# Graph layers with two layer norms: four of ten dense rows' second sums on ScalarE, and a one-row last slot

## Chip, cores and metric

One core of one Trainium2 chip. The time is device microseconds of the whole program; less is better.

## The reference, cut to what matters

A graph of 50000 nodes with 128 features and 12500 edges. A first message layer gives x1 = layernorm(x + mean of messages), then two relational attention layers (eight relations, softmax over each node's incoming edges) and x2 = layernorm(x1 + h2):

```python
x = _layernorm(x + _L0_gnn_ref(x, edge_attr_128, src, dst, ...), axis=-1)
x = _layernorm(x + _L1_gnn_ref(x, W, att_q, att_k, bias, edge_index, edge_type_8), axis=-1)
```

Most nodes have no incoming edge. For such a row the messages are zero and each attention layer gives relu(bias), so the output is layernorm(layernorm(x) + relu(bias of layer 1)). This is the dense work: it runs over all 50000 rows beside the edge work, and rows with edges are overwritten at the end.

## The kernel before

**Dense work.** The rows are cut into 39 slots (c = 0 to 38) of 10 rows on each of 128 partitions (BR = 10) and a last slot c = 39 (BC) with one row on 80 partitions. Three buffers of `stage` hold slots in turn. Step k does the first layer norm of slot k and the second of slot k - 1:

- VectorE `bulk_first(k)`: five pair statistics (one instruction gives count, mean and summed square deviation of two rows) of slot k, once its load has landed.
- VectorE `bulk_shift(k)`: waits for `b_norm1`, adds relu(bias) to all rows of slot k - 1.
- VectorE `bulk_second(k)`: five pair statistics of slot k - 1; then `b_sum`.
- ScalarE `root(k)`: square root of all twenty sums; then `b_sd`.
- VectorE `bulk_scales(k)`: a reciprocal and a product give scale `rs` and bias `nm`; then `b_rs`.
- ScalarE `bulk_norm(k, 0)`: ten norms (one per row, scale and bias) of slot k, then `b_norm1`; `bulk_norm(k, 1)`: ten of slot k - 1, then `b_norm2`.
- SyncE `bulk_step(k)`: waits for `b_norm2`, stores slot k - 1, waits for the store, loads slot k + 2 in its place.

In the before kernel the last slot is treated as ten rows on every engine but in its load and store.

**Edge work.** 98 tiles of 128 edges in 14 groups of 7 (NG = 14, G = 7). First stage: groups 0 to 13 with dense steps 3 to 16. Then two attention layers (j = 0, 1). A layer runs over 112 slots n; for n < 98, group g = n // 7, r = n % 7 + 1. In slot n:

- VectorE makes mask r of group g (`STT(masked(n), ...)`, into one of three buffers; it waits until TensorE has used the mask three slots back), then the dense piece of that r (`bulk_piece`), then, in some slots, a piece of the softmax (`chain`, slots 38 to 45 and 66 to 73) and every fourth slot from 50 the weighting and running sum of a group (`weighted`).
- TensorE multiplies mask r with the relation's matrix (`product`; relation 0 goes first in a group, from the rows themselves). At slots 4, 9, 14, ... it turns the rows of the next group (`turn_rows`, needs the gather), and two slots later makes its key scores (`key_scores`).
- ScalarE copies turned rows (`rows_T`), key scores (`keys_out`) and, at r = 7, the group's products (`products_out`) out of PSUM, and does the dense norms and roots at fixed r; from slot 50 also `relu_sums`, `h1_out` and `fill`.
- GpSimd gathers the rows of all groups in one run (98 indirect transfers, each group into its own place).

Each engine's queue runs in program order. Layer 0 has dense steps k = 18 to 30 in groups 0 to 12, layer 1 steps 33 to 39 in groups 0 to 6 and the last, 40, in group 7. Steps 17, 31 and 32 lie ahead of the layers' slots. Before, the dense pieces stand so:

- VectorE: r 1 and 2 `bulk_first`, 3 shift, 4 `bulk_second` and sums, 6 scales.
- ScalarE: r 2 and 3 the second norms of step k - 1 (five each), 4 root, 6 and 7 the first norms of step k.
- SyncE: its step at r 4.

## Time and profile before

| | |
|---|---|
| median of 3 runs | 950.29 us (945.18 to 953.65) |
| profiled execution | 952.45 us, span 950.7 us |
| busy: PE, DVE, ACT, POOL | 678.6, 750.2, 614.4, 581.1 us |
| layer 0, its slots | about 335 to 616 us |
| layer 1, its slots | about 632 to 913 us |

PE is TensorE, DVE VectorE, ACT ScalarE, POOL GpSimd. Times in the trace count from the span's start. In a timeline row stand start, duration, engine, line, operation, written<-read tile, count, and in brackets the idle time before it and who ended it. Instructions of one kind in a row are merged, and successive ones overlap a little, so a pace is read from start to start.

### The profile page before, as it was taken

Reading aid. Unit: us, or ns where it says so; the run is one execution under the profiler, and the core shown is the slowest. Engines: PE = TensorE matmul, PEld = TensorE weight load, DVE = VectorE, ACT = ScalarE, POOL = GpSimd, SP = SyncE. Lnnn points to the kernel's source line nnn. Section 1 sums busy time; section 2 is a strip of 40 time slices with the busy share of each in tenths; the row PEclk is TensorE's granted clock in tenths of the full one; section 3 lists DMA queues with packets and bytes.
Section 4 is the critical chain, followed back from the end, with each engine's and each line's share of the span. In section 5 each row is a group of like instructions: output and inputs, shape, how many; then the busy total and the mean of one; then the engine's idle time right before and its main releaser. Section 6 shows DMA issues by size and latency. Waiting matters only on the chain.

```text
span 950.7 us, 10537 instructions
## 1 busy us (share of the span) xinstructions
PE 678.6 (71%) x3022; PEld 431.6 (45%) x3022; DVE 750.2 (79%) x1445; ACT 614.4 (65%) x1425; POOL 581.1 (61%) x506
## 2 busy tenths in 40 slices
PE   2646756656475499997998689649998888678810
PEld 2524544545353355554665345426564455343400
DVE  3488877887679678978998899688978887899950
ACT  1569898989799766656566687566665564334450
POOL 4777777777771488887700000088888866557774
PEclk9657696777767589999998999869999999889955
DMA  8276657656563422323553454523231521142210
GB/s 226 87 215 200 204 161 220 206 170 200 161 186 123 157 71 97 101 70 125 195 148 114 127 185 142 166 87 110 69 129 45 184 70 48 42 113 81 70 41 29
DMA packets 87764, 122.96 MB, mean 129 GB/s; under 512 B 14188, under 2 KB 66854, under 8 KB 87707
## 3 DMA queue, kind: packets, MB, share of 16 engines
q1 hardware_dynamic: 69483, 99.36, 33.4%
q0 software_dynamic: 15680, 21.55, 8.1%
q10 hardware_dynamic: 2544, 1.38, 0.7%
q8 instruction: 24, 0.39, 0.2%
q14 instruction: 33, 0.27, 0.1%
HBM read 87.79 MB, written 45.05 MB: 140 GB/s over the span
## 4 chain that ended last, share of the span: by engine, by line
DVE 27%; POOL 22%; issue 17%; PE 14%; ACT 11%; DMA 7%; SPq 1%; POOLq 0%; DVEq 0%; ACTq 0%
POOL xs L471 16%; DVE ys L1145 5%; PE ps_y L727 5%; DVE work L1320 5%; POOL xd L471 4%; ACT stage L808 4%; DVE st L1073 4%; DMA xs<-h_table,posI 3%; DVE ys L1292 2%; DVE opT L1320 2%; PE ps_t L689 2%; PE ps_t L588 2%; ACT xd L824 1%; POOL out L540 1%; DMA xs<-x_table,posI 1%
## 5 line engine op out<-in xcount | busy, mean ns | idle before, releaser
L808 ACT ACTIVATE stage<-stage,nm,rs 128x128 f32<-128x128 f32 x800 | 319.9, 483 | 19.1 <-DVE nm L1069 19.1
L727 PE MATMUL ps_y<-work,wr 128*128 128x512 f32 (+1 forms) x528 | 231.8, 572 | 20.0 <-DVE work L1320 20.0
L471 POOL DMA_INDIRECT xs<-h_table,posI x98 | 130.1, 1327 | 169.3 <-DMA h_table<-ys 139.7
L471 POOL DMA_INDIRECT xs<-x_table,posI x98 | 128.0, 1306 | 61.1 <-DMA x_table<-xd 31.5
L1073 DVE BATCH_NORM_STATS2 st<-stage 128x6 f32<-128x256 f32 x400 | 144.6, 418 | 25.1 <-DMA stage<-in_x 23.8
L1320 DVE SCALAR_TENSOR_TENSOR work<-typB,xs 128x896 f32<-128x896 uint8 x132 | 142.6, 1087 | 18.4 <-ACT xs L773 9.0
L727 PEld LDWEIGHTS ps_y<-work,wr 128*128 128x128 f32 x528 | 100.4, 200 | 115.1 <-issue 70.8
L540 POOL DMA_INDIRECT out<-xd,outI x98 | 107.8, 1100 | 55.0 <-issue 27.7
L471 POOL DMA_INDIRECT xs<-in_x,srcI x98 | 103.7, 1058 | 43.3 <-issue 28.7
L471 POOL DMA_INDIRECT xd<-in_x,dstG x98 | 109.7, 1119 | 29.9 <-issue 28.6
L727 PE MATMUL ps_y<-opT,wr 128*128 128x512 f32 (+1 forms) x256 | 114.9, 573 | 10.3 <-DVE opT L1320 10.3
L824 ACT ACTIVATE xd<-xd,nm,rs 128x128 f32<-128x128 f32 x196 | 78.3, 481 | 18.1 <-DVE nm L1069 18.1
L1145 DVE TENSOR_TENSOR_SCAN ys<-sameB,tail,ys 128x896 f32<-128x896 uint8 x39 | 81.2, 2081 | 0.9
L1320 DVE SCALAR_TENSOR_TENSOR opT<-typB,xs 128x896 f32<-128x896 uint8 x64 | 69.7, 1089 | 10.1 <-PE ps_y L727 8.1
L727 PEld LDWEIGHTS ps_y<-opT,wr 128*128 128x128 f32 x256 | 48.3, 200 | 55.1 <-issue 33.5
L773 ACT ACTIVATE xs<-ps_t 128x896 f32<-128x896 f32 x28 | 25.7, 916 | 73.1 <-PE ps_t L677 73.1
L1086 DVE TENSOR_TENSOR stage<-stage,relu_row 128x1280 f32<-128x1280 f32 x40 | 59.4, 1485 | 6.9 <-ACT stage L808 6.9
L1068 DVE RECIPROCAL rs<-sd 128x20 f32<-128x20 f32 (+3 forms) x55 | 15.3, 277 | 57.5 <-ACT sd L802 57.1
L727 PE MATMUL ps_y<-xs,wr 128*128 128x512 f32 (+1 forms) x112 | 51.9, 589 | 2.2 <-ACT xs L773 2.2
L717 PEld LDWEIGHTS ps_k<-wqk,xs 128*128 128x128 f32 x392 | 47.9, 192 | 6.2 <-issue 0.6
L623 PE MATMUL ps_y<-opT,mixed 128*128 128x512 f32 (+1 forms) x56 | 36.2, 737 | 15.3 <-ACT opT L773 15.3
L905 ACT ACTIVATE ys<-ys,bcol 128x896 f32<-128x896 f32 x28 | 29.2, 1043 | 27.4 <-DVE tail L1148 27.0
(208 smaller groups left out, 1027.6 us busy)
## 6 DMA issues: line engine op xcount, KB each, us to landing
stage<-in_x SPq DMA_DIRECT2D x39, 640.0 KB, 4.2
out<-stage SPq DMA_DIRECT2D x39, 640.0 KB, 3.0
xs<-alpha_rows SPq DMA_DIRECT2D x28, 448.0 KB, 4.7
x_table<-xd SPq DMA_DIRECT2D x14, 448.0 KB, 3.0
h_table<-ys SPq DMA_DIRECT2D x14, 448.0 KB, 3.4
work<-in_src SPq DMA_DIRECT2D x13, 448.0 KB, 5.5
ys<-in_edge_attr SPq DMA_DIRECT2D x6, 896.0 KB, 9.2
sameB<-same_rows SPq DMA_DIRECT2D x42, 112.0 KB, 3.7
```

The lines of the kernel that those rows point to most:

```text
L471: nc.gpsimd.indirect_dma_start(out=buf[:, t, :], out_offset=None, in_=table, in_offset=bass.IndirectOffsetOnAxis(ap=idx[:, t:t + 1], axis= ...
L540: nc.gpsimd.indirect_dma_start(out=out, out_offset=bass.IndirectOffsetOnAxis(ap=outI[:, t:t + 1], axis=0), in_=xd[:, t, :], in_offset=None ...
L623: pe.matmul(ps_y[:, 0, lo:hi], m_node, opT[:, 0, lo:hi], start=True, stop=False)
L717: mm = pe.matmul(ps_k[:, t * R:(t + 1) * R], xs[:, g * G + t, :], wqk[:, 1, j * R:(j + 1) * R], start=True, stop=True)
L727: mm = pe.matmul(ps_y[:, u, lo:hi], wr[:, r, :], rows, start=(r == 0), stop=(r == R - 1))
L808: ins = a.activation(slot(c)[:, r, :], slot(c)[:, r, :], ACT.Identity, bias=nm[:, h, n:n + 1], scale=rs[:, h, n:n + 1])
L824: ins = a.activation(buf[:, g * G + t, :], buf[:, g * G + t, :], ACT.Identity, bias=nm[:, h, o + t:o + t + 1], scale=rs[:, h, o + t:o + t ...
L905: a.activation(cols_of(ys, g), cols_of(ys, g), ACT.Relu, bias=bcol[:, 5 + j:6 + j]).then_inc(g_act[j], 1)
L1073: return v.bn_stats(st[:, h, o:o + 2, :].rearrange("p a c -> p (a c)"), both)
L1086: T.of(TT(slot(k - 1), slot(k - 1), mid(relu_row[:, 1, :], BR), ALU.add))
L1145: ins = scan(cols_of(ys, g), sameB[:, n % 2, :], cols_of(ys, g), tail[:, 0:1] if g else 0.0, ALU.mult, ALU.add)
L1320: STT(masked(n), typB[:, m % 2, :], float(r), cols_of(xs, g), ALU.is_equal, ALU.mult).then_inc(m_mask[j], 1)
```

## The change

Four things. (1) In steps 18 to 39 the last four rows (SQ = 4) of slot k - 1 get no pair statistic. ScalarE squares them with a running sum (`bulk_squares`), from the shift on (`b_shift`), before the root, into the place where the summed square deviation would stand. (2) That is the deviation only if the shifted row's mean is zero, so relu(bias) has its mean taken off once in the prologue; those rows' second norm then has no bias. (3) The order in a layer's group: VectorE's scales go from r 6 to 7. ScalarE has squares at 4, root at 5, second norms at 7 (five) and at r 1 of the next group (five), first norms, all ten, at r 2. SyncE's step goes from r 4 to 2. (4) The last slot: one statistic, one row shifted and one norm in place of ten rows.

```diff
@@ -193,6 +196,12 @@
             b = c % SLOTS
             return stage[:, b * BR * D:(b + 1) * BR * D].rearrange("p (r d) -> p r d", d=D)
 
+        def rows_of(c):
+            return 1 if c == BC else BR
+
+        def squared(k):
+            return SQ if K_H[0] < k <= BC else 0
+
         def grp(t, g):
             return t[:, g * G:g * G + G, :]
 
@@ -247,6 +256,7 @@
         pro = sem("dve_steps")
 
         b_sum = sem("b_sum"); b_sd = sem("b_sd"); b_rs = sem("b_rs"); b_norm1 = sem("b_norm1"); b_norm2 = sem("b_norm2")
+        b_shift = sem("b_shift"); b_sq = sem("b_sq")
 
         p_step = sem("p_step"); p_row = sem("p_row"); p_ready = sem("p_ready")
 
@@ -419,7 +429,7 @@
                     bulk_step(k)
                 for n in range(SLOTS_ALL):
                     g, r = n // (R - 1), n % (R - 1) + 1
-                    if r == 4 and K_M[j] + g <= K_E[j]:
+                    if r == 2 and K_M[j] + g <= K_E[j]:
                         bulk_step(K_M[j] + g - 1)
                     if n in STORE:
                         alpha_store(j, STORE.index(n))
@@ -803,21 +813,36 @@
 
             def bulk_norm(k, half, rows=range(BR)):
                 h, c, done = k % 2, k - half, (b_norm1, b_norm2)[half]
-                for r in rows:
-                    n = half * BR + r
-                    ins = a.activation(slot(c)[:, r, :], slot(c)[:, r, :], ACT.Identity,
-                                       bias=nm[:, h, n:n + 1], scale=rs[:, h, n:n + 1])
-                if rows[-1] == BR - 1:
-                    ins.then_inc(done, 1)
-
-            def bulk_step(k, first=True, second=True):
+                for r in rows[:max(0, rows_of(c) - rows[0])]:
+                    n, row = half * BR + r, slot(c)[:, r, :]
+                    if half and r >= BR - squared(k):
+                        ins = a.activation(row, row, ACT.Identity, scale=rs[:, h, n:n + 1])
+                    else:
+                        ins = a.activation(row, row, ACT.Identity, bias=nm[:, h, n:n + 1], scale=rs[:, h, n:n + 1])
+                    if r == rows_of(c) - 1:
+                        ins.then_inc(done, 1)
+
+            def bulk_squares(k):
+                act.wait_ge(b_shift, k - K_H[0])
+                for r in range(BR - SQ, BR):
+                    ins = a.activation(junk[:, r - BR + SQ, :], slot(k - 1)[:, r, :], ACT.Square,
+                                       accum_out=st[:, k % 2, BR + r, 2:3])
+                ins.then_inc(b_sq, 1)
+
+            def bulk_root(k, first=True):
                 act.wait_ge(b_sum, k + 1)
-                root(k, 0 if first else BR, 2 * BR if second else BR).then_inc(b_sd, 1)
+                if squared(k):
+                    act.wait_ge(b_sq, k - K_H[0])
+                root(k, 0 if first else BR, 2 * BR).then_inc(b_sd, 1)
+
+            def bulk_step(k, first=True):
+                if squared(k):
+                    bulk_squares(k)
+                bulk_root(k, first)
                 act.wait_ge(b_rs, k + 1)
                 if first:
                     bulk_norm(k, 0)
-                if second:
-                    bulk_norm(k, 1)
+                bulk_norm(k, 1)
 
             def norm_rows(buf, g, h, o, done, each=False):
                 for t in range(G):
@@ -925,25 +950,26 @@
                     norm_rows(xd, g, g % 2, XD, f_rows[2], each=g == NG - 1)
 
                 k = K_M[j] - 1
-                act.wait_ge(b_sum, k + 1)
-                root(k, 0, 2 * BR).then_inc(b_sd, 1)
+                if squared(k):
+                    bulk_squares(k)
+                bulk_root(k)
                 rows_T(0)
                 act.wait_ge(b_rs, k + 1)
-                bulk_norm(k, 0, range(BR // 2))
+                bulk_norm(k, 1, range(BR // 2))
                 for n in range(SLOTS_ALL):
                     g, r = n // (R - 1), n % (R - 1) + 1
                     k = K_M[j] + g
-                    if n == 0:
-                        bulk_norm(k - 1, 0, range(BR // 2, BR))
-                    if k <= K_E[j] and r in (2, 3):
-                        bulk_norm(k - 1, 1, range((r - 2) * BR // 2, (r - 1) * BR // 2))
-                    if k < K_E[j] and r == 4:
-                        act.wait_ge(b_sum, k + 1)
-                        root(k, 0, 2 * BR).then_inc(b_sd, 1)
-                    if k < K_E[j] and r in (6, 7):
-                        if r == 6:
-                            act.wait_ge(b_rs, k + 1)
-                        bulk_norm(k, 0, range((r - 6) * BR // 2, (r - 5) * BR // 2))
+                    if k <= K_E[j] and r == 1:
+                        bulk_norm(k - 1, 1, range(BR // 2, BR))
+                    if k <= K_E[j] and r == 2:
+                        bulk_norm(k - 1, 0)
+                    if k < K_E[j] and r == 4 and squared(k):
+                        bulk_squares(k)
+                    if k < K_E[j] and r == 5:
+                        bulk_root(k)
+                    if k < K_E[j] and r == 7:
+                        act.wait_ge(b_rs, k + 1)
+                        bulk_norm(k, 1, range(BR // 2))
                     for s in range(NG):
                         if TURN[s] + 2 == n:
                             keys_out(s)
@@ -1050,6 +1076,9 @@
             dve.wait_ge(par_in, 16 * N_PAR)
             T.of(TT(bcol[:, 2:3], bcol[:, 0:1], bcol[:, 1:2], ALU.add))
             T.step(TS(relu_row[:], relu_row[:], 0.0, None, ALU.max))
+            T.step(v.tensor_reduce(b_mean[:], relu_row[:, 1, :], AX.X, ALU.add))
+            T.step(TS(b_mean[:], b_mean[:], 1.0 / D, None, ALU.mult))
+            T.step(TS(relu_row[:, 1, :], relu_row[:, 1, :], b_mean[:, 0:1], None, ALU.subtract))
             dve.sem_inc(bsum_r, 1)
             carried()
             T.step(STT(t0[:], pre[:], ps_s[0:TL, 0:1], t0[:], ALU.mult, ALU.add))
@@ -1064,9 +1093,10 @@
             dve.sem_inc(prol_d, 1)
 
             def scales(k, lo, hi):
-                dev, mean, r_, n_ = sd[:, k % 2, lo:hi], st[:, k % 2, lo:hi, 1], rs[:, k % 2, lo:hi], nm[:, k % 2, lo:hi]
-                T.step(v.reciprocal(r_, dev))
-                return STT(n_, mean, -1.0, r_, ALU.mult, ALU.mult)
+                T.step(v.reciprocal(rs[:, k % 2, lo:hi], sd[:, k % 2, lo:hi]))
+                if hi == 2 * BR:
+                    hi -= squared(k)
+                return STT(nm[:, k % 2, lo:hi], st[:, k % 2, lo:hi, 1], -1.0, rs[:, k % 2, lo:hi], ALU.mult, ALU.mult)
 
             def pair_stats(h, o, rows):
                 both = rows.rearrange("p a d -> p d a")
@@ -1078,18 +1108,34 @@
 
             def bulk_first(k, pairs=range(BR // 2)):
                 dve.wait_ge(bulk_in[k % SLOTS], 16 * (k // SLOTS + 1))
+                if k == BC:
+                    if 0 in pairs:
+                        T.of(single_stats(k % 2, 0, slot(k)[:, 0, :]))
+                    return
                 for r in pairs:
                     T.of(pair_stats(k % 2, 2 * r, slot(k)[:, 2 * r:2 * r + 2, :]))
 
             def bulk_shift(k):
                 dve.wait_ge(b_norm1, k)
-                T.of(TT(slot(k - 1), slot(k - 1), mid(relu_row[:, 1, :], BR), ALU.add))
+                rows = slot(k - 1)[:, 0:rows_of(k - 1), :]
+                ins = TT(rows, rows, mid(relu_row[:, 1, :], rows_of(k - 1)), ALU.add)
+                if k <= K_H[0]:
+                    T.of(ins)
+                else:
+                    ins.then_inc(b_shift, 1)
 
             def bulk_second(k, pairs=range(BR // 2)):
                 for r in pairs:
                     if r == 0:
-                        T.wait()
-                    T.of(pair_stats(k % 2, BR + 2 * r, slot(k - 1)[:, 2 * r:2 * r + 2, :]))
+                        if k <= K_H[0]:
+                            T.wait()
+                        else:
+                            dve.wait_ge(b_shift, k - K_H[0])
+                    if k - 1 == BC:
+                        T.of(single_stats(k % 2, BR, slot(k - 1)[:, 0, :]))
+                        return
+                    if 2 * r < BR - squared(k):
+                        T.of(pair_stats(k % 2, BR + 2 * r, slot(k - 1)[:, 2 * r:2 * r + 2, :]))
 
             def bulk_sums():
                 T.wait()
@@ -1116,7 +1162,7 @@
                 elif n == 4:
                     bulk_second(k)
                     bulk_sums()
-                elif n == 6:
+                elif n == R - 1:
                     bulk_scales(k)
 
             def row_stats(buf, g, h, o):
```

## Rows read from the trace of the kernel before

**Rows 1.** The page: busy time by engine; the chain that ended last, by engine.
```profile
PE 678.6 (71%) x3022; PEld 431.6 (45%) x3022; DVE 750.2 (79%) x1445; ACT 614.4 (65%) x1425; POOL 581.1 (61%) x506
...
DVE 27%; POOL 22%; issue 17%; PE 14%; ACT 11%; DMA 7%; SPq 1%; POOLq 0%; DVEq 0%; ACTq 0%
```

**Rows 2.** Windows, both layers (columns: engines' busy us (instructions), granted clock, DMA share, GB/s).
```profile
335.00:418.00 83.00, 79.27 (x306) 47.05 (x307) 69.32 (x114) 53.86 (x133) 68.36 (x49) 0.97 0.31 96
418.00:508.00 90.00, 82.79 (x359) 51.28 (x358) 78.66 (x133) 57.42 (x131) 48.42 (x40) 0.96 0.42 132
508.00:616.00 108.00, 84.87 (x327) 50.78 (x325) 93.53 (x140) 72.32 (x164) 0.00 (x0) 0.94 0.51 153
632.00:701.00 69.00, 67.76 (x258) 40.06 (x259) 60.13 (x99) 46.22 (x114) 56.50 (x42) 0.97 0.29 93
701.00:773.00 72.00, 61.79 (x237) 36.13 (x235) 59.28 (x103) 42.90 (x98) 58.74 (x44) 0.95 0.33 108
```

**Rows 3.** Tile stage: ScalarE's norms and VectorE's shift (ns, first and last start).
```profile
L808 ACT ACTIVATE stage<-stage,nm,rs x800: 477/482/514, 34.2 to 768.1; 128x128 f32<-128x128 f32 x160
...
L1086 DVE TENSOR_TENSOR stage<-stage,relu_row x40: 1475/1483/1529, 38.2 to 758.2; 128x1280 f32<-128x1280 f32 x40
```

**Rows 4.** Timeline of ScalarE, layer 0, end of group 3, start of 4.
```profile
399.51 0.22 ACT L773 ACTIVATE opT<-ps_k 128x56 f32<-128x56 f32 x1 [1.35 <-PE ps_k L717]
399.62 2.02 ACT L808 ACTIVATE stage<-stage,nm,rs 128x128 f32<-128x128 f32 x5
401.55 0.90 ACT L773 ACTIVATE ys<-ps_y 128x896 f32<-128x896 f32 x1
402.34 2.02 ACT L808 ACTIVATE stage<-stage,nm,rs 128x128 f32<-128x128 f32 x5
```

**Rows 5.** Timeline of VectorE, group 4: mask, shift, mask, five pair statistics; a later wait.
```profile
402.72 1.07 DVE L1320 SCALAR_TENSOR_TENSOR work<-typB,xs 128x896 f32<-128x896 uint8 x1
403.71 1.48 DVE L1086 TENSOR_TENSOR stage<-stage,relu_row 128x1280 f32<-128x1280 f32 x1
405.12 1.08 DVE L1320 SCALAR_TENSOR_TENSOR work<-typB,xs 128x896 f32<-128x896 uint8 x1
406.12 1.74 DVE L1073 BATCH_NORM_STATS2 st<-stage 128x6 f32<-128x256 f32 x5
...
417.03 1.10 DVE L1073 BATCH_NORM_STATS2 st<-stage 128x6 f32<-128x256 f32 x3 [3.38 <-DMA stage<-in_x]
```

**Rows 6.** Timeline of TensorE, group 4: relation-0 product, later products, key scores.
```profile
400.92 1.67 PE L727 MATMUL ps_y<-xs,wr 128*128 128x512 f32 x4
...
406.19 3.17 PE L727 MATMUL ps_y<-work,wr 128*128 128x512 f32 x8
...
409.20 1.62 PE L717 MATMUL ps_k<-wqk,xs 128*128 128x8 f32 x14
```

**Rows 7.** Queue of SyncE: the load of a dense slot.
```profile
412.56 0.33 SPq L335 DMA_DIRECT2D stage<-in_x  x1
```

**Rows 8.** Timeline of TensorE: waits for gathered rows, and the product after one.
```profile
417.52 1.09 PE L677 MATMUL ps_t<-identS,xs 128*128 128x128 f32 x7 [2.08 <-DMA xs<-x_table,posI]
418.40 3.19 PE L727 MATMUL ps_y<-xs,wr 128*128 128x512 f32 x4
...
774.17 0.96 PE L677 MATMUL ps_t<-identS,xs 128*128 128x128 f32 x7 [1.28 <-DMA xs<-h_table,posI]
```

**Rows 9.** Window around the product after that wait (columns as Rows 2).
```profile
418.00:421.50 3.50, 3.50 (x10) 1.86 (x9) 3.50 (x6) 2.86 (x6) 2.89 (x3) 0.54 0.05 12
```

**Rows 10.** Timeline of VectorE: first and thirteenth shift of layer 0, seventh of layer 1.
```profile
339.94 1.49 DVE L1086 TENSOR_TENSOR stage<-stage,relu_row 128x1280 f32<-128x1280 f32 x1
...
571.02 1.49 DVE L1086 TENSOR_TENSOR stage<-stage,relu_row 128x1280 f32<-128x1280 f32 x1
...
738.70 1.48 DVE L1086 TENSOR_TENSOR stage<-stage,relu_row 128x1280 f32<-128x1280 f32 x1
```

**Rows 11.** ScalarE's groups by form: the shortest on 128x128 numbers.
```profile
L773 ACT ACTIVATE ys<-ps_t 128x128 f32<-128x128 f32 x14 | 3.8, 269 | 0.0
```

More of the change, by code:

```diff
@@ L65, in graph_layers @@
     SLOTS = 3
+    SQ = 4
     K_A = 3
@@ L94, in graph_layers @@
     XD, XS = 2 * BR, 2 * BR + GS
-    assert BR % 2 == 0
+    assert BR % 2 == 0 and SQ % 2 == 0
     assert 0 < K_E[1] - K_M[1] < NG and SUMS[HA] > STORE[1] + 2
@@ L151, in graph_layers @@
         nm = sb("nm", [P, 2, W])
+        b_mean = sb("b_mean", [P, 1])
+        junk = sb("junk", [P, SQ, D], U8)
         ps_y = ctx.enter_context(nc.psum_tensor("ps_y", [P, 2, 1024], F32))
```

## Prediction, made before the change was run

> **What bounds the kernel now.** I read the page's busy shares first, then the windows, then the three timelines side by side for one group. VectorE is the busiest engine over the span and ScalarE has a third of it free [rows 1], which invites moving statistics from one to the other. The windows say where that could pay: in the first half of a layer TensorE is busy 79.27 of 83.00 us, and VectorE is idle 13.7, 11.3 and 14.5 us in layer 0's three windows and 8.9 and 12.7 in layer 1's [rows 2]. So both engines are near the bound in turn, and neither alone. The gathers bound a third: TensorE waits 2.08 us for gathered rows at 417.5 and 1.28 at 774.2 [rows 8]. Compute that is faster ahead of 774 in layer 1 can gain at most that 1.28, and compute that is slower loses all but it. All seven groups of layer 1 with dense work lie ahead of it.
>
> The order of the three engines is what matters for the rest. In slot r of a group VectorE makes mask r, then its dense piece. TensorE's products may be up to three masks behind. ScalarE's queue holds turns, key scores and products to copy, so it moves with TensorE.
>
> **The change part by part.** Prices per step: five norms take 1.93 us (399.62 to 401.55) [rows 4], so ten take 3.86 and a step's twenty 7.7 [rows 3, 4]; copying the products out 0.8 [rows 4]; a mask 1.0, the shift 1.4, a pair statistic 0.33 (five in 1.74) [rows 5]; one relation's product 1.5 (two in 3.17), key scores 1.5 [rows 6], a turn 1.05 [rows 8].
>
> 1. Statistics. Steps 18 to 39 drop two of five pair statistics: 0.67 us of VectorE each, 22 steps, 14.7 us, of which 13 steps (8.7 us) are in layer 0's groups and 7 in layer 1's (4.7 us), behind the gathers. Steps 31 and 32 lie between and beside the layers.
>
> 2. Squares. Four per step on ScalarE. No row has one with a running sum. The nearest below is a plain copy of 128x128 at 0.27 us, the nearest above a norm at 0.48 [rows 11, 3] plus an instruction of some 0.2 to put the sum away: 1.1 to 2.7 us a step. I take 2. From the end of the shift VectorE needs 1.0 + 1.0 for mask and sums of slot 4 and 3.0 for three masks before it asks for the root, 5 us, so squares and root (0.3) are hidden at either price; without that cover they would cost up to 22 x 2.7 = 59 us. The Trainium skill's page "ScalarE: Activation LUTs", section "Rules for kernel authors", speaks against the move: it wants a multiplication on VectorE, not on ScalarE. By rows it is true of the work (0.67 us become 1.1 to 2.7), and by that alone the sum would be a loss; but neither number is on the path, so it changes no term.
>
> 3. The order of the norms. This is the part that costs. Before, step k's ten first norms stood in slots 6 and 7 of its group and the shift that waits for them in slot 3 of the next: VectorE never waited for them in a layer. Now the scales come one slot later, ScalarE does the second norms first (five in slot 7, five in slot 1) and all first norms in slot 2; the shift is in slot 3. From scales to shift VectorE has 1.0 + 1.0 + 1.0 + 0.67 + 1.0 = 4.7 us of its own; ScalarE has 7.7 + 0.8 = 8.5 and must also have seen TensorE's last product. The wait takes the place of nothing: behind it in VectorE's queue are all later masks, and TensorE lives on those.
>
> Group 4 of layer 0 shows the size. ScalarE's row at 402.34 is where slot 2's norms start. Put the other five second norms and ten first norms there: 402.34 + 1.93 + 3.86 = 408.1 against a shift that started at 403.71 [rows 4, 5]. VectorE stands 4.4 us. TensorE had three masks in hand and the relation-0 product at 400.92; the third ends 1.5 after 406.19, at 407.7 [rows 6]. The next mask is there at 408.1 + 1.4 + 1.0 = 410.5: TensorE starves 2.8 us.
>
> As a period, where TensorE bounds: now eight products, 12.0, and 7/5 of a turn and key scores, 3.6: 15.6 us a group. After: from the end of a group's last product 0.8 + 1.93 + 3.86 + 1.4 + 1.0 = 9.0 to the mask of slot 4, 0.5 until the following mask, four products 6.0, some 2.0 of turns and scores: 17.5, and 1 more where ScalarE must copy a turn or key scores ahead of the first norms. So +2 to +3 a group.
>
> I laid out layer 0 by these prices, each queue in its order, and each group from the one ahead. The thirteen shifts start before at 340, 356, 369, 389, 404, 421, 443, 465, 481, 502, 532, 555 and 571 [rows 10], which shows the first and the last; laid out, at 343, 361, 380, 400, 419, 437, 459, 483, 503, 528, 558, 582 and 601. TensorE's own delay is smaller in the early groups: its products of group 4 come 13 us late, then the gather wait of 2.1 goes and with it VectorE's 3.4 us wait for a dense slot [rows 5, 8], 11.6 remain. The stretch with the softmax chain is neutral; groups 7 to 9 lose 2 to 5 each, since ScalarE's sums and row copies also stand among the norms. Layer 0: +30, less the last group's 0.67: **+29 us**.
>
> Layer 1 has the same times 296.6 us later up to its seventh shift at 738.70 [rows 10]: +16. There the last dense slot comes in: one row of ten. VectorE saves 1.3 on its first statistics, 1.2 on the shift, 1.3 on second statistics; ScalarE 9 + 9 norms, 7 us, and the first-norm wait of that group is gone. Some 2 us of the delay go there, and 1.3 into the gather wait at 774: 16 - 2 - 1.3 = 12.7, **+12 us**.
>
> 4. Early load. In group 4 the second norms would end at 404.3 (402.34 + 1.93) instead of after slot 3's five, so that the load issued at 412.56 [rows 7] comes some 5 us sooner and the statistic behind it, which waited 3.38 us at 417.03 [rows 5], starts without a wait. Such waits are part of VectorE's idle time and are counted in the layout. Moved past alpha and row stores on SyncE's queue, the dense load waits for nothing new: its turn is two slots earlier and its norms are too.
>
> 5. The prologue's three small operations on a 128x128 bias and a column: 0.6 us by the 0.2 to 0.3 us that such operations take, beside matmuls; nothing at the end, at most 0.6.
>
> Sum: 29 + 12 = 41 us on the profiled execution's 952.5, which is 2.2 above the median; on the median 950.3 + 41 = **991 us**.
>
> **The rivals.** (a) All idle absorbs it. Summing the static waits read as in group 4 gives 61 us in layer 0's thirteen groups and 31 in layer 1's seven. If VectorE's present idle takes them in full: layer 0, 61 - 8.7 - 39.5 = +13; layer 1, 31 - 4.7 - 21.6 - 3.8 (last slot) - 1.3 = 0. 963 us. Against it: some of that idle is waits for TensorE that stay or fall at another place.
>
> (b) Faster. The mechanism is ScalarE being through with its twenty norms when VectorE reaches slot 3. It decides at 4.7 us from scales to first norms, or wherever VectorE has other work there. Then layer 0 keeps the 8.7 and the 3.4 of the dense load, layer 1 the 1.3 of the gather wait: 950.3 - 13 = 937. For it: ScalarE idles a third of the windows. Against: twenty norms at 0.39 cannot be put into 4.7.
>
> (c) TensorE's clock. After the 2.08 us wait the next product took 3.19 us for four matmuls against 1.67 in group 4, at a granted clock of 0.54 (mostly the 1.2 GHz level); over that half layer it was 0.97 (2.4 GHz) [rows 6, 8, 9, 2]. The layout has some fifteen starved stretches of 2 to 4 us, each perhaps dearer by 1.5, of which I would put two thirds or more on the path: 991 + 15 to 22, 1010 us. The Trainium skill's "TensorE: Matmul & The Clock Gate" says idleness throttles the array to half and activity releases it; the rows agree.
>
> (d) Squares need another function table than the root, so that each step loads twice: dearer than (c), above 1010.
>
> (e) Gains and waits cancel, 950.
>
> **How the numbers follow.** Likeliest: the layout, 991, chance 0.55. (a) 0.15, (c) 0.15, (d) 0.03: slower in all of these. (b) 0.07, (e) 0.05. Range 963 to 1010, from (a) to (c). A kernel within 1% (9.5 us, about what a measurement of this one can tell from none) 0.05; faster 0.07; slower 0.88.
>
> **What would show it.** After the change VectorE's shift has a wait on ScalarE's norm of 3 to 8 us in nearly each group, 50 us or more together; TensorE's products wait for masks in slot 4; the pair statistics number 44 fewer beside the last slot's; waits for the dense slot's load are gone in the layers; the second layer's turn at 774 no longer waits for the gather. Wrong would be: shifts without a wait (then b), waits beside an unchanged TensorE (a), or a ScalarE that is full between shift and root (d).

## The result and the profile after

The changed kernel takes **1033.54 us** (median of 4, 1032.39 to 1036.11) against 951.37 us (945.18 to 953.65, 4 runs) measured beside it: a ratio of 1.0894 with an interval of 1.0854 to 1.0934. It is 9% slower. The forecast was 991 us, in a range of 963 to 1010. The side was right, the size was not: +82 us where +41 was forecast. The profiled execution took 1032.41 us with a span of 1030.6, against a span of 950.7 before, so the trace has 79.9 us to explain.

The page of the changed kernel, busy time by engine and the chain that ended last, against [rows 1]:

```profile
PE 714.8 (69%) x3022; PEld 450.5 (44%) x3022; DVE 734.4 (71%) x1396; ACT 627.4 (61%) x1583; POOL 554.9 (54%) x506
...
DVE 29%; PE 27%; ACT 23%; POOL 9%; issue 7%; DMA 3%; SPq 1%; DVEq 0%; POOLq 0%; ACTq 0%
```

VectorE lost 15.8 us of work, as intended. TensorE has the same 3022 matmuls and is busy 36.2 us longer with them. ScalarE's share of the chain doubled, from 11% to 23%, though it is only 13 us busier: it is waited for, not full.

VectorE's groups by line say for what. The last column is idle time ahead of the group and who ended it; the shift stood at 6.9 us before:

```profile
L1103 DVE BATCH_NORM_STATS2 st<-stage 128x6 f32<-128x256 f32 x346 | 126.3, 418 | 12.2 <-DMA stage<-in_x 11.2
L1121 DVE TENSOR_TENSOR stage<-stage,relu_row 128x1280 f32<-128x1280 f32 (+1 forms) x40 | 58.5, 1461 | 103.7 <-ACT stage L821 103.7
```

The shift now waits 103.7 us for ScalarE's norms, 97 more than before. One group shows how. First ScalarE, then VectorE, layer 0, group 3 (start, duration):

```profile
397.71 0.22 ACT L783 ACTIVATE opT<-ps_k 128x56 f32<-128x56 f32 x1 [1.97 <-PE ps_k L727]
397.83 3.94 ACT L821 ACTIVATE stage<-stage,nm,rs 128x128 f32<-128x128 f32 x10
403.38 0.31 ACT L828 ACTIVATE junk<-stage 128x128 uint8<-128x128 f32 x1 [1.61 <-DVE stage L1121]
```
```profile
396.97 1.08 DVE L1366 SCALAR_TENSOR_TENSOR opT<-typB,xs 128x896 f32<-128x896 uint8 x1
401.80 1.55 DVE L1121 TENSOR_TENSOR stage<-stage,relu_row 128x1280 f32<-128x1280 f32 x1 [3.75 <-ACT stage L821]
403.27 1.08 DVE L1366 SCALAR_TENSOR_TENSOR work<-typB,xs 128x896 f32<-128x896 uint8 x1
404.27 1.08 DVE L1103 BATCH_NORM_STATS2 st<-stage 128x6 f32<-128x256 f32 x3
```

VectorE has made mask 3 at 398.05 and stands. ScalarE's ten first norms start at 397.83, because the key scores of the group's slot 1 had to be copied out first, and end at 401.77. The shift starts 0.03 us later, and with it all later masks. TensorE is the third to stop. Its rows in groups 3 and 4:

```profile
399.12 1.67 PE L737 MATMUL ps_y<-opT,wr 128*128 128x512 f32 x4
404.41 3.35 PE L737 MATMUL ps_y<-work,wr 128*128 128x512 f32 x4 [3.62 <-DVE work L1366]
...
423.98 2.60 PE L737 MATMUL ps_y<-work,wr 128*128 128x512 f32 x4 [2.56 <-DVE work L1366]
426.38 3.00 PE L727 MATMUL ps_k<-wqk,xs 128*128 128x8 f32 x14
429.23 3.33 PE L737 MATMUL ps_y<-opT,wr 128*128 128x512 f32 x4
432.35 4.50 PE L737 MATMUL ps_y<-work,wr 128*128 128x512 f32 x8
```

After the gap, a product of four matmuls takes 3.35 us, not 1.67. In group 4 four steps in a row are slow (the last, two products in one row, takes 4.50 us, not 3.17). In both layers TensorE has fourteen gaps of 1.8 us or more ahead of a product that waits for a mask, and behind twelve of them the product takes some 2.6 us or more, not 1.67. Windows over 10 us of group 4 and over group 3's slow product (the number after POOL's is the granted clock):

```profile
422.00:432.00 10.00, 8.02 (x22) 5.45 (x23) 6.48 (x10) 3.52 (x16) 7.90 (x7) 0.64 0.24 78
404.40:407.70 3.30, 3.29 (x5) 1.55 (x6) 3.05 (x5) 0.26 (x2) 2.63 (x2) 0.50 0.04 10
```

A granted clock of 0.50 is the 1.2 GHz level of the two. Layer 0's windows, against [rows 2], show the same over longer stretches: a lower clock in all three (0.97, 0.96, 0.94 before), less work done by both engines in the first two, and less by VectorE in the third.

```profile
335.00:418.00 83.00, 72.19 (x259) 41.49 (x260) 57.22 (x90) 48.79 (x144) 66.53 (x55) 0.93 0.25 79
418.00:508.00 90.00, 73.41 (x254) 43.87 (x253) 60.52 (x103) 46.28 (x129) 38.42 (x34) 0.83 0.34 111
508.00:616.00 108.00, 85.63 (x327) 50.92 (x326) 81.20 (x125) 69.32 (x185) 0.00 (x0) 0.87 0.40 119
```

The delay comes from the layers alone. VectorE's shifts, the thirteenth of layer 0 and the seventh and eighth of layer 1, against [rows 10]:

```profile
619.19 1.49 DVE L1121 TENSOR_TENSOR stage<-stage,relu_row 128x1280 f32<-128x1280 f32 x1 [3.26 <-ACT stage L821]
...
818.54 1.49 DVE L1121 TENSOR_TENSOR stage<-stage,relu_row 128x1280 f32<-128x1280 f32 x1 [2.11 <-ACT stage L821]
...
839.90 0.29 DVE L1121 TENSOR_TENSOR stage<-stage,relu_row 128x128 f32<-128x128 f32 x1 [1.26 <-ACT stage L821]
```

Layer 1's first turn comes at 679.83, 50.7 us later than before. The seventh shift of layer 1 comes 79.8 later (818.54 against 738.70): layer 1 adds 29.1 up to there, and 29.2 by the end of the program.

### The profile page after: what moved, and what is told of

It reads as the page before. It is cut to its first block, busy times and chain, and to the rows that moved or that the text cites. A ratio compares the mean times of both kernels' runs of the same rounds, so it can differ in the third digit from the quotient of the medians.

```text
span 1030.6 us, 10669 instructions
## 1 busy us (share of the span) xinstructions
PE 714.8 (69%) x3022; PEld 450.5 (44%) x3022; DVE 734.4 (71%) x1396; ACT 627.4 (61%) x1583; POOL 554.9 (54%) x506
## 4 chain that ended last, share of the span: by engine, by line
DVE 29%; PE 27%; ACT 23%; POOL 9%; issue 7%; DMA 3%; SPq 1%; DVEq 0%; POOLq 0%; ACTq 0%
PE ps_y L737 15%; ACT stage L821 13%; DVE work L1366 5%; DVE ys L1191 5%; POOL xs L481 4%; DVE st L1103 4%; POOL xd L481 3%; DVE stage L1121 3%; PE ps_k L727 3%; DVE opT L1366 2%; DVE ys L1338 2%; ACT ys L783 2%; PE ps_t L687 2%; PE ps_t L699 1%; POOL out L550 1%
## 5 line engine op out<-in xcount | busy, mean ns | idle before, releaser
L821 ACT ACTIVATE stage<-stage,nm,rs 128x128 f32<-128x128 f32 x694 | 279.4, 483 | 18.0 <-DVE nm L1099 18.0
L737 PE MATMUL ps_y<-work,wr 128*128 128x512 f32 (+1 forms) x528 | 248.9, 606 | 37.9 <-DVE work L1366 37.9
L481 POOL DMA_INDIRECT xs<-h_table,posI x98 | 119.1, 1215 | 231.7 <-DMA h_table<-ys 202.2
L737 PEld LDWEIGHTS ps_y<-work,wr 128*128 128x128 f32 x528 | 107.0, 214 | 143.4 <-issue 79.7
L481 POOL DMA_INDIRECT xs<-x_table,posI x98 | 116.9, 1193 | 63.8 <-DMA x_table<-xd 34.2
L737 PE MATMUL ps_y<-opT,wr 128*128 128x512 f32 (+1 forms) x256 | 130.3, 638 | 20.0 <-DVE opT L1366 20.0
L1103 DVE BATCH_NORM_STATS2 st<-stage 128x6 f32<-128x256 f32 x346 | 126.3, 418 | 12.2 <-DMA stage<-in_x 11.2
L1121 DVE TENSOR_TENSOR stage<-stage,relu_row 128x1280 f32<-128x1280 f32 (+1 forms) x40 | 58.5, 1461 | 103.7 <-ACT stage L821 103.7
L737 PEld LDWEIGHTS ps_y<-opT,wr 128*128 128x128 f32 x256 | 53.2, 221 | 71.5 <-issue 39.1
L783 ACT ACTIVATE xs<-ps_t 128x896 f32<-128x896 f32 x28 | 25.6, 915 | 94.9 <-PE ps_t L687 94.9
L1096 DVE RECIPROCAL rs<-sd 128x20 f32<-128x20 f32 (+3 forms) x55 | 15.3, 278 | 63.7 <-ACT sd L812 63.3
L727 PEld LDWEIGHTS ps_k<-wqk,xs 128*128 128x128 f32 x392 | 50.7, 202 | 6.5 <-issue 1.2
L737 PE MATMUL ps_y<-xs,wr 128*128 128x512 f32 (+1 forms) x112 | 50.7, 578 | 2.2 <-ACT xs L783 2.2
L930 ACT ACTIVATE ys<-ys,bcol 128x896 f32<-128x896 f32 x28 | 29.2, 1044 | 35.7 <-DVE tail L1194 35.4
L607 PE MATMUL ps_k<-wqk,ys 128*128 128x8 f32 x196 | 28.1, 278 | 29.3 <-issue 22.0
```

Source lines behind the costliest of these rows:

```text
L481: nc.gpsimd.indirect_dma_start(out=buf[:, t, :], out_offset=None, in_=table, in_offset=bass.IndirectOffsetOnAxis(ap=idx[:, t:t + 1], axis= ...
L727: mm = pe.matmul(ps_k[:, t * R:(t + 1) * R], xs[:, g * G + t, :], wqk[:, 1, j * R:(j + 1) * R], start=True, stop=True)
L737: mm = pe.matmul(ps_y[:, u, lo:hi], wr[:, r, :], rows, start=(r == 0), stop=(r == R - 1))
L783: return a.activation(o, i_, ACT.Copy)
L821: ins = a.activation(row, row, ACT.Identity, bias=nm[:, h, n:n + 1], scale=rs[:, h, n:n + 1])
L930: a.activation(cols_of(ys, g), cols_of(ys, g), ACT.Relu, bias=bcol[:, 5 + j:6 + j]).then_inc(g_act[j], 1)
```

## The experiments

In all kernels the part of the diff that isn't named is as in the kernel it starts from. "Before" in the ratios is the kernel before as measured beside the run (948 to 950 us). "Shift wait" is the idle time ahead of VectorE's shifts, from the groups by line.

| label | kernel | us | ratio (interval) | shift wait, us |
|---|---|---|---|---|
| e1_order_no_squares | changed, no squares | 1037.05 | 1.0924 (1.0881 to 1.0967) | 105.5 |
| e8_norm_order_alone | before, new order of norms only | 1035.63 | 1.0908 (1.0848 to 1.0968) | 108.0 |
| e2_old_order_squares | changed, old order | 949.77 | 0.9997 (0.9973 to 1.0022) | 6.8 |
| e3_last_slot_only | before, one-row last slot | 949.92 | 1.0004 (0.9981 to 1.0028) | 6.6 |
| e13_old_order_root_later | e2, root in slot 5 | 948.99 | 1.0003 (0.9979 to 1.0028) | 7.2 |
| e4_halves_swapped | changed, first norms ahead | 952.86 | 1.0024 (0.9998 to 1.005) | 18.5 |
| e7_shift_one_later | changed, shift in slot 4 | 980.64 | 1.031 (1.0259 to 1.0362) | 49.1 |
| e5_fill_after | changed, 12 dummy matmuls | 1063.84 | 1.1194 (1.1137 to 1.125) | 102.2 |
| e6_fill_before | before, 12 dummy matmuls | 1022.45 | 1.0762 (1.0703 to 1.0821) | 9.5 |
| e9_small_fill_after | changed, 5 | 1023.99 | 1.0777 (1.0747 to 1.0807) | 99.2 |
| e10_small_fill_before | before, 5 | 968.84 | 1.0218 (1.0174 to 1.0262) | 9.1 |
| e11_three_fill_after | changed, 3 | 1018.98 | 1.0728 (1.0684 to 1.0771) | 99.6 |
| e12_three_fill_before | before, 3 | 959.8 | 1.01 (1.0063 to 1.0137) | 7.2 |

### Which part of the change costs

**e1_order_no_squares**: the changed kernel with all ten rows' second statistics on VectorE.

```diff
-    SQ = 4
+    SQ = 0
...
```


> The changed kernel with SQ = 0: order of the norms and the one-row last slot as changed, but VectorE makes all five pair statistics again and ScalarE squares nothing. Theory A (the order: first norms come last, the shift waits for them, and TensorE starves): stays at 1030 to 1050 us, since squares are off the path, with the two pair statistics (0.67 us a step) added to the loop. Rival S (the squares make ScalarE late): falls below 990. Wait of the shift on ScalarE's norm: A 90 us or more, S under 50.

It is as slow as the changed kernel; the two intervals overlap. The squares don't cost the 82 us.

**e8_norm_order_alone**: the kernel before with the norms alone reordered: five second norms in slot 6, five in slot 1 of the next group, all ten first norms in slot 2. Root (4), scales (6) and SyncE's step (4) stay in their old places, there are no squares, and the last slot has ten rows. The five norms ahead of the layer's slots are exchanged as well, here and in e2 and e4.

```diff
-                    if n == 0:
-                        bulk_norm(k - 1, 0, range(BR // 2, BR))
-                    if k <= K_E[j] and r in (2, 3):
-                        bulk_norm(k - 1, 1, range((r - 2) * BR // 2, (r - 1) * BR // 2))
+                    if k <= K_E[j] and r == 1:
+                        bulk_norm(k - 1, 1, range(BR // 2, BR))
+                    if k <= K_E[j] and r == 2:
+                        bulk_norm(k - 1, 0)
...
-                    if k < K_E[j] and r in (6, 7):
-                        if r == 6:
-                            act.wait_ge(b_rs, k + 1)
-                        bulk_norm(k, 0, range((r - 6) * BR // 2, (r - 5) * BR // 2))
+                    if k < K_E[j] and r == 6:
+                        act.wait_ge(b_rs, k + 1)
+                        bulk_norm(k, 1, range(BR // 2))
```


> The kernel before with the norms' order alone: second norms at r 6 (five) and r 1 (five), all first norms at r 2; root stays at 4, scales at 6, SyncE at 4, no squares, ten rows in the last slot. Theory A: 1010 to 1040 us, since the first norms still follow products out by 1.93 + 3.86 us. Rival P (the later scales matter as well): 975 to 1005.

The order of the norms alone, put into the kernel before, gives the whole slowdown, in the range that the theory of the order gave. The later scales, which e8 doesn't have, aren't needed for it.

**e2_old_order_squares**: the changed kernel with before's order (first norms in slots 6 and 7, second in 2 and 3, squares and root in 4, scales in 6, SyncE in 4).

> The changed kernel with the order of before: squares and root at r 4, first norms at 6 and 7, second at 2 and 3, scales at 6, SyncE at 4. Squares and one-row last slot stay. Theory A: 930 to 950 us, no wait of the shift. Rival S: 985 or more, since 88 squares with their reads stay on ScalarE (some 40 us).

No difference from the kernel before, though VectorE has 54 pair statistics fewer. Where part of the saved work goes, VectorE's rows of e2 show, layer 0's scales of groups 0 to 2 and 8:

```profile
346.36 0.28 DVE L1097 RECIPROCAL rs<-sd 128x20 f32<-128x20 f32 x1 [1.27 <-ACT sd L812]
362.45 0.28 DVE L1097 RECIPROCAL rs<-sd 128x20 f32<-128x20 f32 x1 [1.91 <-ACT sd L812]
377.57 0.28 DVE L1097 RECIPROCAL rs<-sd 128x20 f32<-128x20 f32 x1 [2.19 <-ACT sd L812]
...
490.00 0.28 DVE L1097 RECIPROCAL rs<-sd 128x20 f32<-128x20 f32 x1 [3.38 <-ACT sd L812]
```

VectorE waits for the root. From 335 to 600 these waits sum to 9.4 us, against 2.4 in the kernel before: 7.0 of the 8.7 us of statistics saved there became waits.

**e3_last_slot_only**: e2 with `SQ = 0`, so that the one-row last slot and the prologue's three operations are all that is left of the change.

> The kernel before with only the one-row last slot (SQ = 0, old order). Both theories: 946 to 951 us; the saving (some 4 us of VectorE) lies in layer 1 ahead of the last gather, which leaves 1.3 us of it. Were it near 960 or more, something else of the change costs.

Nothing measurable.

**e13_old_order_root_later**: e2 with the root one slot behind the squares, to see whether the saving can be had.

```diff
...
+                    if k < K_E[j] and r == 5:
                         bulk_root(k)
...
```


> The old order with the squares, and the root one slot behind them (slot 5, not 4), to see whether the 13 to 15 us of statistics saved can be had when ScalarE doesn't have to stand for VectorE's sums ahead of slot 4's copies. If ScalarE's stand for the sums is what eats the saving: 938 to 946. If the saving is lost because VectorE only waits elsewhere (for TensorE, the gathers and the root): 946 to 953. If the root one slot later makes the scales wait and the first norms in slots 6 and 7 late: 953 to 970.

948.99 us: again the kernel before. VectorE's wait for the root over the whole run is 77.4 us, against 73.5 in e2 and 57.1 before. No placement tried here turned the saved statistics into time, and no kernel of this study beats the kernel before.

### Is it the distance from norms to shift

**e4_halves_swapped**: the changed kernel with the two kinds of norm exchanged: five first norms in slot 7, five in slot 1, all ten second norms in slot 2. Root, squares, scales and SyncE stay in their new places.

```diff
-                        bulk_norm(k - 1, 1, range(BR // 2, BR))
+                        bulk_norm(k - 1, 0, range(BR // 2, BR))
                     if k <= K_E[j] and r == 2:
-                        bulk_norm(k - 1, 0)
+                        bulk_norm(k - 1, 1)
...
-                        bulk_norm(k, 1, range(BR // 2))
+                        bulk_norm(k, 0, range(BR // 2))
```


> The changed kernel with the two halves swapped: first norms five at r 7 and five at r 1, second norms all ten at r 2. Everything else as changed. Theory A: the first norms are through some 4.7 us after the scales, when VectorE reaches the shift, so nearly all of the 82 us goes: 935 to 965 us, waits of the shift under 15 us in all. Rival S: 1000 or more. Rival P (the later places of scales and root cost): 980 to 1000.

Same work on each engine, same slots: 952.86 us, and 18.5 us of shift waits where under 15 were expected. So it is not ScalarE's load, nor the later scales, nor SyncE's earlier step, but which ten norms stand directly ahead of the shift.

**e7_shift_one_later**: the changed kernel with shift, second statistics and squares, and root one slot later.

```diff
-                    if k < K_E[j] and r == 4 and squared(k):
+                    if k < K_E[j] and r == 5 and squared(k):
                         bulk_squares(k)
-                    if k < K_E[j] and r == 5:
+                    if k < K_E[j] and r == 6:
...
-                elif n == 3:
+                elif n == 4:
                     bulk_shift(k)
-                elif n == 4:
+                elif n == 5:
                     bulk_second(k)
```


> The changed kernel with the shift at r 4 in place of 3, second statistics and squares at 5, root at 6; scales stay at 7. VectorE makes one more mask (1.0 us) before it waits, so TensorE has four products in hand and not three. If only the wait of VectorE counts (W): some 20 x 1.0 us less, 1010 us. If what counts is TensorE's starving (theory C: 1.5 us less of it, and the clock stays up): 960 to 990 us.

One mask (1.0 us) more between norms and shift gives back 53 us. The time is in theory C's range, but that doesn't decide for C: the shift waits fell by 54.6 us, 2.7 a group where 1.0 was expected, and why they fell so far isn't shown. Shift waits and times of three kernels stand near one line: in e4 18.5 us of waits cost 3.3 (which the interval does not separate from nothing), in e7 49.1 cost 32.6, in the changed kernel 103.7 cost 82.2. So a microsecond of wait costs 0.9 to 1.0, from (32.6 - 3.3) / (49.1 - 18.5) = 0.96 and (82.2 - 32.6) / (103.7 - 49.1) = 0.91, and the line meets zero at about 15 us. These prices include what TensorE's clock adds: its later products (tiles work and opT) take 344.2, 355.5 and 379.2 us in the three kernels.

### How much of it is TensorE's clock

The fillers are matmuls of 128x256 numbers with no user; each stands as two instructions in the trace. They stand ahead of product 4 in the twenty groups with dense work, where TensorE waits for VectorE's late mask. They write the other half of `ps_y`, and so first wait until ScalarE has copied the last group's products out of it.

```diff
+                        if r == 4 and K_M[j] + g < K_E[j]:
+                            pe.wait_ge(m_ys[j] if g else q_used, g if g else j + 1)
+                            for _ in range(12):
+                                pe.matmul(ps_y[:, 1 - g % 2, 0:2 * P], ident, wr[:, 0:2, :], start=True, stop=True)
                         product(g, r, n)
```

**e5_fill_after**, **e6_fill_before**: twelve of them in the changed kernel, and in the kernel before as a control.

> The changed kernel, and TensorE makes twelve extra 128x256 matmuls (2.6 us at 2.4 GHz) whose result nobody reads, ahead of the product of r 4 in the twenty groups with dense work, where it now starves. Theory C (a good third of the 82 us is the clock that falls in the starved stretches): although TensorE gets 52 us more work, the kernel becomes faster, 1000 to 1020 us, and the four matmuls behind the starved stretch take 1.7 us again, not 3.3. Rival W (the clock is a sign, not a cost; the waits alone make the 82): 1033 or more.

> The control: the same twelve extra matmuls at the same place in the kernel before, which has no starved stretch there. Theory C and W alike: slower, by up to 2.6 us in each group that TensorE bounds: 970 to 1000 us.

Neither came out. The filler was mis-sized: twelve take 5.4 us, twice what was meant, and are longer than the gap. They cost 74 us in the kernel before and 30 in the changed one. But TensorE's products got faster. The groups of the changed kernel, then of e5:

```profile
L737 PE MATMUL ps_y<-work,wr 128*128 128x512 f32 (+1 forms) x528 | 248.9, 606 | 37.9 <-DVE work L1366 37.9
L737 PE MATMUL ps_y<-opT,wr 128*128 128x512 f32 (+1 forms) x256 | 130.3, 638 | 20.0 <-DVE opT L1366 20.0
```
```profile
L737 PE MATMUL ps_y<-work,wr 128*128 128x512 f32 (+1 forms) x528 | 225.3, 558 | 12.7 <-DVE work L1370 12.7
L737 PE MATMUL ps_y<-opT,wr 128*128 128x512 f32 (+1 forms) x256 | 115.9, 578 | 6.6 <-DVE opT L1370 6.6
```

Together 379.2 us became 341.2, for the same products; the kernel before has 346.7, and 336.9 with the same twelve.

**e9_small_fill_after**, **e10_small_fill_before**: five instead of twelve. (Both expectations speak of 40 groups, which is wrong: they are twenty, so twelve took 115.6 / 20 = 5.8 us busy, and what fillers cost in the kernel before is 3.7 us a group.)

> The changed kernel with five dummy products of 256 columns on TensorE ahead of product 4 of each dense group, not twelve. The twelve took 5.3 us (from the run before: 115.6 us for 40 groups of the two layers), more than the 2.9 to 4.9 us that TensorE stands there, so that run mixed a cost of the filler with what the clock gave back. Five should take 2.2 us and fit into the gap. Clock theory: the products behind it are back at about 1.7 us for four matmuls instead of 3.3, the products of work and opT sum to 340 to 355 us instead of 379, and the time is 1000 to 1018. Wait theory (the late shift alone is the cost, the slow products lie beside it): the fillers change nothing, 1030 to 1037. Filler theory (the gap isn't free, since the next group's work can't move): 1045 to 1065.

> The same five dummy products in the kernel before, as the control of what they cost by themselves. Twelve cost 74 us in 40 groups, of which 5.3 us a group were their own length. By length five cost 5/12 of it, 31 us: 975 to 985. If the kernel before too has a gap there that they fill or a clock that they hold (its slow products sum to some 6 us over the full pace): 955 to 972. In either case the difference from the changed kernel with the same fillers, set against 82 us without them and 41 us with twelve, is what the gap and the clock give back: clock theory 25 to 45 us left, wait theory 50 to 60, filler theory 82.

**e11_three_fill_after**, **e12_three_fill_before**: three.

> The changed kernel with three dummy products ahead of product 4 in each of the twenty dense groups. Five took 2.3 us and in nine of the twenty groups ended later than the mask for product 4 was there, so that the 9.5 us they gave back is a lower end for what the clock costs. Three take 1.4 us and should end inside the gap nearly everywhere. Clock theory (a good part of the difference is TensorE at its lower level after the gap): the time falls further than with five, 1008 to 1022. Wait theory (the clock's loss lies beside the wait of the shift and is worth some 10 us at most): 1022 to 1034. If three are too few to hold the clock, the products of work and opT stay above 365 us together and the time stays at 1030 to 1036.

> The control: the same three in the kernel before. Five cost 19 us, 0.95 a group, under half their length. Three should cost 3/5 of that or less: 950 to 962. If they cost nothing the kernel before has gaps of 1.4 us there anyway: 947 to 952.

The expectations disagree. With five, the time of 1023.99 us is in no theory's range, and the 55 us left between e9 and e10 are what the wait theory had (50 to 60); with three, 1018.98 is in the clock theory's range, with 59 us left between e11 and e12. Both controls, 968.84 and 959.8, are in their ranges. So the clock is a cost, and the smaller part of the 82 us.

Adding useless work makes the changed kernel faster: by 9.5 us with five and by **14.6 us** with three, which cost the kernel before 19 and 12; the ratios' intervals, 1.0747 to 1.0807 and 1.0684 to 1.0771, lie below the changed kernel's 1.0854 to 1.0934. The filler gives 14.6 us back, so the clock is worth at least about that. If the fillers cost in the changed kernel what they cost in the other, which is unlikely where they lie in a gap, it is 14.6 + 11.7 = 26 us; what it costs where the fillers don't hold it comes on top, within the 36.2 us that TensorE is busier. The traces agree: from the first to the thirteenth shift of layer 0 and from the first to the seventh of layer 1 the changed kernel takes 276.4 and 128.7 us, e11 268.0 and 121.7, together 15.3 less. The later products (work and opT) take 31.2 us less (379.2 against 348.0), so about half of their slowness was on the path. Where it comes from can be read. TensorE in e11, group 4, to be held against the changed kernel's rows at 423.98 to 429.23:

```profile
427.00 1.46 PE L761 MATMUL ps_y<-wr,identS 128*128 128x256 f32 x6
429.73 1.77 PE L737 MATMUL ps_y<-work,wr 128*128 128x512 f32 x4 [1.27 <-DVE work L1370]
431.34 1.62 PE L727 MATMUL ps_k<-wqk,xs 128*128 128x8 f32 x14
432.82 1.75 PE L737 MATMUL ps_y<-opT,wr 128*128 128x512 f32 x4
```

and the granted clock over 10 us from 427.5, which was 0.64 in the changed kernel:

```profile
427.50:437.50 10.00, 8.73 (x36) 5.26 (x35) 9.43 (x15) 4.19 (x16) 8.17 (x7) 1.00 0.25 80
```

From group 4's shift to group 5's, layer 0, it is 23.4 us in the changed kernel (421.43 to 444.80) and 18.3 in e11 (427.18 to 445.51). Layer 1 has the same pair: 23.4 (769.58 to 792.94) and 18.3 (760.95 to 779.28). These two periods are 10 of the 15 us. The rows of group 4 have them: its four slow steps take 5.1 us more than in e11 (there 1.77, 1.62, 1.75 and, behind the rows shown, 3.17). Group 3 gives one more and a check: in layer 0 the product behind its gap takes 3.35 us with and without fillers, and the period to group 4 is 19.6 in both; in layer 1 it takes 3.35 in the changed kernel and 1.77 in e11, and the period goes from 19.7 (749.93 to 769.58) to 18.0 (742.94 to 760.95). Not each slow product counts: group 2's took 2.86 us in the changed kernel and 1.77 in e11, and its period is 21.1 in both.

## Why the prediction was right or wrong

**What bounds the kernel**: right for the kernel before. The gather wait at 774 is gone in the changed kernel, as said. TensorE's 13.7 us of waits on gathered rows of layer 1 are all in front of that layer's first turn.

**1, statistics**: the size was right (44 pair statistics fewer, and 10 more from the last slot: 400 to 346). Its worth was not: the layout credited 8.7 and 4.7 us. e1 against the changed kernel gives 3.5 us, which the intervals don't separate from nothing, and e2 against e3 gives none.

**2, squares**: hidden, as forecast. The tile's view has the price that the trace of before lacked:

```profile
L828 ACT ACTIVATE junk<-stage x88: 292/294/332, 345.2 to 828.4; 128x128 uint8<-128x128 f32 x88
L828 ACT ACTIVATION_READ_ACCUMULATOR junk<-stage x88: 185/187/226, 345.4 to 828.6; 128x1 f32 x88
```

A square and its put-away are issued every 0.29 us, so that four take 1.2 us: near the lower bound of 1.1, not the 2 taken. No table load is added (ten in both kernels), so rival (d) is out. The rule of the Trainium skill's page "ScalarE: Activation LUTs", section "Rules for kernel authors", that wants a multiplication on VectorE, gives the right sign of the work (0.67 us became 1.2) and is worth nothing in time here, since neither number is on the path.

**3, the order**: the mechanism is shown, by e8 (it alone gives the loss) and e4 (the exchange of the two kinds of norm takes it away). The size of the waits was right too. The static sums, 61 us in layer 0 and 31 in layer 1's seven groups, were measured as 62.2 and 33.3 (34.5 with the eighth shift). That sums read off the old timeline came out so near is partly luck: group by group they are less near. Group 4's 4.4 us was 5.66, TensorE's 2.8 us of starving there was 2.56 (423.98), and the first five laid-out shifts, 343, 361, 380, 400 and 419, came at 342.8, 361.0, 380.7, 401.8 and 421.4.

**The step that failed** is how much of these waits is absorbed. The layout let existing idle time take 32 of the 61 us in layer 0 and 15 of 31 in layer 1. Of 62.2, layer 0 passed on 50.7, of 34.5 layer 1 passed on 29.2. Three terms of it can be named:

- TensorE's clock. The sum took each product at 1.5 us, and left the clock to rival (c) with fifteen stretches of 1.5 us. The mechanism is as (c) has it: a granted clock of 0.50 over the product behind a gap of 3.62 us, and 1.00 in group 4 once fillers lie in its gap. The Trainium skill's "TensorE: Matmul & The Clock Gate", section "What's actually happening", says the same, that the array is throttled by default and activity releases it. The clock's worth is at least about 14.6 us (e11), near (c)'s 15 to 22, and the fifteen stretches are near the fourteen gaps of 1.8 us or more. But it isn't spread over them: two periods, group 4's of each layer, hold 10 us of it. From group 4's shift to the next the layout had 18 us (419 to 437), which took 23.4, and 18.3 with fillers. With (c)'s term the sum would have been 1006 to 1013, still too low.
- "The stretch with the softmax chain is neutral." It isn't. From shift 444.80 two groups take 50.4 us, against 44.2 before (shifts at 420.70 and 464.93) and 46 in the layout (437 to 483). The 6.2 us over before are as much as the two shift waits in it, though not group by group (3.1 and 3.1 us longer, with waits of 2.2 and 4.1):

```profile
470.38 1.49 DVE L1121 TENSOR_TENSOR stage<-stage,relu_row 128x1280 f32<-128x1280 f32 x1 [2.18 <-ACT stage L821]
495.20 1.49 DVE L1121 TENSOR_TENSOR stage<-stage,relu_row 128x1280 f32<-128x1280 f32 x1 [4.06 <-ACT stage L821]
```

Layer 1 enters the same stretch: from its sixth shift to its seventh it takes 25.6 us (792.94 to 818.54), where the layout has 22, and 26.4 in e11. That is 3.6 more.

- Layer 1's "some 2 us" for the last slot and 1.3 for the gather wait. The seventh shift is 79.8 us late, the eighth 81.7 (839.90 against 758.21) and the whole span 79.9 us longer: what was given back behind the eighth shift had been lost ahead of it.

Of the 39 us missing (79.9 less 41) these are 14.6, 4.4 + 3.6 and 3.3. The rest, some 13 us, no run splits. Some 3 of them lie between the layers: from the thirteenth shift of layer 0 to the first of layer 1 the changed kernel takes 70.7 us, against 65.5 before and 2 more in the layout. Where the others lie can be seen in e11, whose fillers mostly hold the clock: layer 0's first to thirteenth shift take 268 us where the layout had 258, of which 5 are in the softmax stretch and 2.3 behind the eighth shift; the other periods differ by -1.4 to +1.2.

**4, the early load**: dense load waits fell from 23.8 us [rows 5 shows one of them] to 11.2, and inside the layers none is left. That the earlier step of SyncE did this isn't shown: e8, which has the step in its old place, and e6, which is the kernel before made slower by fillers, have no such wait inside the layers either, while e4, with the step in its new place, has 13.6 us there, as the kernel before has 13.2. So a slower loop is enough to remove them. It was worth nothing, since the engine that no longer waits for the load waits for the norms.

**5, the prologue**: its three operations on VectorE take 0.73 us (285, 153 and 288 ns, at 19.7 to 20.5 us), near the 0.6 forecast, and e3 and e2, which have them, are as fast as the kernel before.

**The rivals**: (a), idle absorbs all, is out by the waits passed on; (b) and (e) by the sign; (d) by the table loads; (c) is a part of the truth.

## What to carry to other kernels

When a step is reordered, count from the last instruction a waiting engine needs to the wait itself, in the waiting engine's own work, and compare with what the other engine has queued in between; exchanging two equal blocks on ScalarE moved this kernel by 8%. If two engines feed each other through a short ring of buffers, take a new static wait as passed on for the most part (here 0.8 of it in each layer, what TensorE's clock adds included), not as half absorbed by idle time that the profile shows elsewhere. If the wait also starves TensorE, price the matmuls behind the gap at the lower clock as well, and look for the place where several of them follow each other.

## What the runs showed of the hardware that was not expected

Three useless matmuls of 256 columns (1.46 us) at the start of each gap made the program 14.6 us faster, by keeping TensorE's granted clock at 1.00 in stretches where it was 0.64. They don't do so in every group: in group 3 of layer 0 a gap of 2.32 us behind them was still followed by a product of 3.35 us, in the same group of layer 1 by one of 1.77. ScalarE's instruction that puts a running sum away takes 187 ns and overlaps with the next square: the pair is issued every 0.29 us, less than a norm with its bias (0.39).
